# Which engine subtracts the softmax's high parts: GpSimd in place of VectorE, in an attention and feed-forward block

## What is computed

```python
x = x + attention(layernorm(x), ctx)   # 32 heads of 128, 4 key/value heads, 8 query heads on each
x = x + ffn(layernorm(x))              # 512 -> 1376 -> 512, gate and up, weights in 4-bit steps of 32
# attention:
scores = einsum('bhgqk,...', q, k) / sqrt(128)      # keys: 128 of the context, 128 of x
attn = softmax(scores)
out = attn @ v;  return out @ Wo
```

## Time and profile before

| | us |
|---|---|
| device time, median of 3 runs | 816.74 (816.33 to 817.72) |
| the profiled execution | 816.17 |
| its span, first to last instruction | 814.4 |

### The profile page before, as it was taken

The page is one execution under the profiler, slowest core; times in us unless marked ns, Lnnn a source line. Parts: engine busy times, 40 slices in busy tenths (PEclk is TensorE's granted clock), DMA queues, the critical chain, the costliest instruction groups (busy, mean ns, idle before and its releaser), DMA issues.

```text
span 814.4 us, 12628 instructions
## 1 busy us (share of the span) xinstructions
PE 774.8 (95%) x4771; PEld 466.9 (57%) x4771; DVE 599.7 (74%) x1110; ACT 434.0 (53%) x941; POOL 242.9 (30%) x374
## 2 busy tenths in 40 slices
PE   9999999999999999999999999999999999941998
PEld 3446476666666666666666666665544444420445
DVE  5976467788777878767778777898777459989531
ACT  5545447555566655655655555555630019782920
POOL 0720323456334366343456434434300000000000
PEclk9999999999999999999999999999999999985999
DMA  9643145766546666555765547888772000000011
GB/s 319 138 137 117 39 90 133 169 130 156 104 105 159 154 140 145 102 130 122 177 139 137 127 98 136 157 180 150 140 119 46 1 0 1 1 0 0 27 39 39
DMA packets 212044, 87.59 MB, mean 108 GB/s; under 512 B 178832, under 2 KB 195472, under 8 KB 211984
## 3 DMA queue, kind: packets, MB, share of 16 engines
q1 hardware_dynamic: 211984, 86.79, 47.3%
HBM read 31.72 MB, written 10.75 MB: 52 GB/s over the span
## 4 chain that ended last, share of the span: by engine, by line
PE 79%; DVE 10%; DMA 4%; POOL 3%; ACT 2%; issue 1%; SPq 1%; ACTq 0%; DVEq 0%; POOLq 0%
PE bank L338 21%; PE bank L514 12%; PE bank L446 12%; PE bank L430 10%; PE bank L418 9%; PE bank L583 7%; PE bank L450 6%; DVE arena L777 3%; DVE stats L1127 1%; DVE arena L1117 1%; DMA arena<-arena 1%; POOL arena L1204 1%; ACT arena L591 1%; POOL arena L1160 1%; DMA arena<-in_ctx_t 1%
## 5 line engine op out<-in xcount | busy, mean ns | idle before, releaser
L338 PE MATMUL bank<-arena 128*128 128x256 f16 (+1 forms) x1872 | 260.1, 292 | 1.1 <-DVE arena L777 1.1
L338 PEld LDWEIGHTS bank<-arena 128*128 128x128 f16 x1872 | 182.9, 98 | 83.3 <-DVE arena L777 1.3
L1160 POOL TENSOR_SCALAR arena<-arena,rsum 128x256 f32<-128x256 f32 x256 | 133.8, 523 | 288.6 <-DVE rsum L836 274.4
L777 DVE SCALAR_TENSOR_TENSOR arena<-bank,arena 128x512 f16<-128x512 f32 x160 | 109.7, 689 | 113.1 <-ACT arena L591 112.9
L777 DVE SCALAR_TENSOR_TENSOR arena<-arena 128x512 f16<-128x512 f32 (+4 forms) x198 | 171.9, 882 | 19.8 <-ACT arena L591 18.9
L591 ACT ACTIVATE arena<-bank 128x512 f16<-128x512 f32 x160 | 94.7, 596 | 159.0 <-PE bank L430 98.9
L591 ACT ACTIVATE arena<-arena 128x512 f16<-128x512 f32 (+4 forms) x173 | 135.4, 807 | 48.8 <-POOL arena L1190 15.0
L634 ACT ACTIVATE arena<-bank,nmax 128x256 f32<-128x256 f32 x256 | 117.9, 472 | 47.6 <-DVE nmax L828 46.0
L446 PE MATMUL bank<-arena 128*128 128x512 f16 x512 | 121.0, 379 | 0.7 <-ACT arena L591 0.7
L514 PE MATMUL bank<-arena 128*128 128x512 f16 x507 | 109.8, 379 | 0.2 <-DVE stats L1058 0.2
L430 PE MATMUL bank<-arena 128*128 128x512 f16 x384 | 93.4, 379 | 2.5 <-DMA arena<-arena 2.5
(11 more groups left out here) (102 smaller groups left out, 503.8 us busy)
## 6 DMA issues: line engine op xcount, KB each, us to landing
arena<-in_w_units SPq DMA_DIRECT2D x33, 256.0 KB, 3.7
w_ready<-arena SPq DMA_DIRECT2D x33, 256.0 KB, 3.2
arena<-in_wq SPq DMA_DIRECT2D x32, 256.0 KB, 3.4
arena<-in_wo SPq DMA_DIRECT2D x32, 256.0 KB, 3.5
arena<-in_x SPq DMA_DIRECT2D x2, 1024.0 KB, 11.6
out<-arena SPq DMA_DIRECT2D x7, 256.0 KB, 2.0
arena<-arena SPq DMA_TRANSPOSE x72, 4.3
arena<-in_wk SPq DMA_DIRECT2D x4, 256.0 KB, 4.8
```

Source lines behind the costliest of these rows:

```text
L338: last = nc.tensor.matmul(bank, a(i, c), b(j, c), start=start and c == 0 and n == 0, stop=stop and c == chunks - 1 and n == 2)
L777: return nc.vector.scalar_tensor_tensor(out=dst, in0=src, scalar=scale, in1=part, op0=ALU.mult, op1=ALU.subtract)
L1160: done = nc.gpsimd.tensor_scalar(p_s[:, t % 2, :, hh, :], p_s[:, t % 2, :, hh, :], rsum[:, t % 2, hh:hh + 1], P_SCALE, ALU.mult, ALU.mult)
```

## The change

p_lower(t), the subtraction that makes the low part of the probabilities, goes from VectorE's program to GpSimd's. On GpSimd it is a tensor_tensor subtraction (on VectorE it was a multiply by 1.0 and subtract in one instruction, with the same result). For t = 0 it stands in slot 26, in front of normalise(1); for the others at the beginning of GpSimd's step, in front of unit_normalise, unit_dequantise, wq_upper and normalise(t+2). It waits for p_hi, and raises p_lo, as before.

```diff
@@ VectorE @@
-            def p_lower(t):
-                dve.wait_ge(p_hi, t + 1)
-                lo(p_16[:, t % 2, 1, :], p_s[:, t % 2].rearrange("p c h t -> p (c h t)"), p_16[:, t % 2, 0, :], 1.0).then_inc(p_lo, 1)
-
...
-                if slot == 26:
-                    p_lower(0)
...
-                if t + 1 < STEPS:
-                    p_lower(t + 1)
@@ GpSimd @@
+            def p_lower(t):
+
+                pool.wait_ge(p_hi, t + 1)
+                nc.gpsimd.tensor_tensor(p_16[:, t % 2, 1, :], p_s[:, t % 2].rearrange("p c h t -> p (c h t)"), p_16[:, t % 2, 0, :],
+                                        ALU.subtract).then_inc(p_lo, 1)
+
...
                 if slot == 26:
+                    p_lower(0)
                     normalise(1)
...
             for t in range(STEPS):
+                if t + 1 < STEPS:
+                    p_lower(t + 1)
                 for v in units_at(t, 1):
                     unit_normalise(v)
```

## The result

| | us |
|---|---|
| device time before, median of 4 runs on the same chip | 816.89 (816.33 to 817.72) |
| device time after, median of 4 runs | 903.03 (902.53 to 903.74) |
| ratio after to before | 1.106, 95% interval 1.1046 to 1.1073 |
| span of the profiled execution, before and after | 814.4 and 900.8 |

The change costs 86.1 us. Forecast were 922 us, with a range of 896 to 943, so the time lies in the range. The loss forecast was 24% too large (106.7 against 86.1).

The account below looks back on a forecast made before the run. TensorE bounds the kernel now; after the change a closed loop through p_lower and the softmax would. Loop +101.0, last group +3.8, head +1.4 and tail +0.5 sum to +106.7 on 816.17 us: forecast 922 us, range 896 to 943.

Parts of the forecast that it names:

- The bound: Attention steps: TensorE sets the pace at 7.82 us a step through 58 of 64 steps; relieving VectorE there gains nothing.
- The loop: p_upper to next p_upper through p_lower and unit work: 18.10 us a pair of steps against TensorE's 15.63; difference +101.0 us.
- The size of p_lower: GpSimd's 128x1024 subtraction: 2.31 us taken, twice the shortest half-width one, with 1.22 and 2.67 as ends.
- the last group's term: Last head group: ln2_apply on VectorE ahead of the rounding adds 7 times 0.54, +3.8 us taken, between 0 and 3.8.
- The bound from below: Shortest p_lower on GpSimd: 2.1 us if 0.2 of the half-width instruction's 1153 ns were fixed, -12 us in the range.
- wq work: Steps k = 7 to 11 of three groups: stretched normalise 3.3 us a group, wq_upper's queue place 1.3; 13.8 in all.
- Head and tail: Before and after the steady steps: +1.4 us from later normalising and rounding, +0.5 from 2.2 less a 1.7 DMA gain.
- rival 4: TensorE, idle about 2.5 us in 18, is granted only 1.2 GHz: 453 us more, 1270 us; chance 0.03.
- Rival 1: GpSimd's 5.5 us of step work fits under 7.82, so only head and tail pay: 818 us; chance 0.04.
- Rival 2: GpSimd subtracts the wide tile at VectorE's 1.22 us, a pair taking 15.92 us: 858 us; chance 0.05.
- Rival 3: Every p_lower takes 2.67 us through contention between GpSimd and VectorE, 20.9 us more: 943 us; chance 0.08.
- Rival 5: p_lower under 1.08 us leaves TensorE the bound, and relieved VectorE counts in the tail: 814 us; chance 0.02.

Follow-up runs that it names:

- e9: Changed kernel with p_lower(0) and p_lower(59) to p_lower(63) back on VectorE, the 58 between on GpSimd behind the unit work: 816.54 us (1.0006).
- e1: Changed kernel with GpSimd's p_lower(t+1) moved behind unit_normalise and unit_dequantise in its step: 823.94 us (1.0086).
- e10: Kernel before, p_lower still on VectorE, with GpSimd made to wait at each step's head until VectorE's p_lower(t+1) is done: 850.13 us (1.0413).
- e3: Changed kernel with p_lower(t+1) ahead of the unit work in even steps only, behind it in odd steps: 866.40 us (1.0607).

## Why the prediction was right, point by point

- **The bound, and why VectorE's relief gains nothing.** Right on the bound: with p_lower off VectorE in 58 steps, e9 takes the time of before within 0.15%, and TensorE is as busy there as before. That a relief would gain nothing follows from this, but no run shows it by itself, as the exclusion gave VectorE more busy time than the move took.
- **The loop.** Right, link by link. The odd step was worked out as 8.47 and is 8.16, the even one as 9.63 and is 9.24; with wo work 9.07 and 8.76, 10.23 and 9.76. The cover that the prediction named (unit work under p_upper) is what e1 restores.
- **The size of p_lower.** This is the term that was mis-sized. The line of p_lower after, min/median/max in ns:

```profile
L1159 POOL TENSOR_TENSOR arena<-arena x64: 2122/2127/2631, 89.8 to 671.8; 128x1024 f16<-128x1024 f32 x64
```

  Taken were 2.31 us (twice the half width) and 0.08 to the next instruction. Measured are 2.13, and the next one starts 2.08 after p_lower's start (424.30 to 426.38), 0.05 before its end. By the earlier trace rows and this row 512 more columns cost 0.97 us and 0.18 are fixed. That is 0.31 a step (2.31 + 0.08 less 2.08), 58 x 0.31 = 18 us of the 25 by which the 58 steps were forecast too long (556.9, with the last group's term, against 650.45 - 118.35 = 532.1). The even steps' ScalarE copies took 0.08 to 0.15 less (some 3 us), and ln2_apply cost 0.18 and not 0.54 a step, in 4 such turns up to p_upper(60) where 7 were counted (3 us). The bound from below in the prediction, 2.1 us, was the better value. The total came nearer than this term by luck: the steps were 25 us too long in the forecast, head and tail 4.6 too short.
- **wq work.** 4.6 us a group forecast, 4.6 measured (8.79, 10.14, 8.80, 10.14, 9.72 against 8.16 and 9.24). 3.3 of it is the stretched normalise, as forecast. The 1.3 put down to wq_upper's place in the queue have the right size, but another way: the rounding starts as soon as the unit is normalised, and wq_upper beside it then lengthens L853 to 0.72 us, in k = 11 the instruction behind it too (1.09 in place of 0.67).
- **Head and tail.** Forecast +1.4 and +0.5, measured +2.0 (118.35 against 116.36) and +4.5 (900.8 - 650.45 against 814.4 - 568.51). In the tail I had counted on a gain of 1.7, the DMA of p_lower(60) falling from 6.0 to 4.3 us. It took 5.6, behind a p_lower of 2.64 us. The chain after:

```profile
651.59 2.64 POOL arena L1159
654.24 5.64 DMA arena<-arena
...
671.84 2.14 POOL arena L1159
674.00 4.24 DMA arena<-arena
```

  p_lower(60) and its DMA cost 1.1 us on this chain. p_lower(62) shut VectorE's nmax out (1.30 in place of 0.17 us at 664.88) ahead of the last exps, 1.1, and p_lower(63) costs 0.9, of 1.1 forecast. Another 1.3 come from TensorE's clock (rival 4).

  At the head, half of the 2.0 is the forecast's path: behind p_lower(0) and normalise(1) the rounding starts at 95.30 in place of 94.33, v_lo with it, and p_upper(1) comes 1.0 later (110.56 against 109.58). p_lower(0) also held an instruction of unit_scales, and TensorE waited 0.22 us for the v_lo behind it. The other half came one step later and was not forecast: p_lower(1) shut out nmax (0.17 us before), for which the exps wait.

```profile
89.77 2.13 POOL L1159 TENSOR_TENSOR arena<-arena 128x1024 f16<-128x1024 f32 x1 [5.57 <-ACT arena L591]
...
90.15 1.77 DVE L843 TENSOR_SCALAR wscale<-amax 128x16 f32<-128x16 f32 x1
...
112.63 1.20 DVE L828 TENSOR_SCALAR nmax<-nraw 128x4 f32<-128x4 f32 x1
```

- **Rival 1, room on GpSimd.** Refuted for the change, and true for e9.
- **Rival 2, VectorE's pace.** Refuted by the duration. e10 is nearly the kernel that it priced, at VectorE's pace with nothing lost at head and tail: 850 us, where the rival said 858.
- **Rival 3, contention.** The exclusion is real, but p_lower's median shows that it hardly lengthens p_lower where the change puts it. VectorE is its victim (L843 above), and time is lost by it only where something on the chain waits for that instruction: in e3, at the head and in the tail. The forecast looked at the wrong side of it. It named the form with two inputs in SBUF; its own row of 116.89, and most of what was shut out here, are TENSOR_SCALAR instructions.
- **Rival 4, the clock.** TensorE's clock did fall. It cost nothing in the 58 steps, and about 1.3 us in the tail. A short stretch after (length; PE, PEld, DVE, ACT, POOL; PEclk, DMA, GB/s), and TensorE in another:

```profile
450.00:454.00 4.00, 4.00 (x13) 1.62 (x12) 2.07 (x4) 2.55 (x7) 2.68 (x4) 0.59 0.46 140
```

```profile
505.11 3.40 PE L446 MATMUL bank<-arena 128*128 128x512 f16 x8 [2.54 <-ACT arena L591]
```

  Eight matmuls that took 1.89 us take 3.40, at 1.2 GHz, after an idle time of 2.54 us, in some of the steps. The turns of the loop stay at 9.76 and 8.76 us through the stretch at 450, as TensorE is not in the loop. In the tail it is on the chain: the clock was 0.73 of full speed from 678 to 681 us and 0.77 from 681 to 685, behind 1.95 us of idle time, and this group of the last project took 1.9 us before:

```profile
680.67 2.94 PE L446 MATMUL bank<-arena 128*128 128x512 f16 x8
```

- **Rival 5, faster.** Refuted.

What is left open: head and tail were given back together, what a VectorE really relieved would be worth was not tried, and how the exclusion picks the winner when both engines start within 0.05 us was not tried.

## What to carry to other kernels

Before a piece of work goes to the engine with the most idle time, write down what is queued behind its new place and who waits for that, and add up the whole turn from an instruction back to the same one of the next step. If this turn is longer than the bound's step, every step pays, whatever the busy shares say. Here the place in the queue decided between 903 and 824 us with the same instructions. And a long GpSimd instruction on SBUF can stop VectorE's TENSOR_SCALAR on SBUF, even on 4 elements a partition, and its subtraction with both inputs in SBUF. A profile shows that as a longer instruction, as busy time and not as idle time, so a moved instruction need not relieve the engine that it left.

## What the runs showed of the hardware

- A GpSimd subtraction of 128x1024 (float32 less float16, into float16) takes 2.13 us, one of 128x512 1.15 us at least; the unit instruction behind p_lower starts 0.05 us before p_lower's recorded end.
- GpSimd and some of VectorE's instructions exclude each other by whole instructions, both ways: VectorE's 0.43 us rounding took 2.23 beside a whole p_lower and 1.26 beside half of one, a 0.17 us one on 16 elements a partition took 1.77, and GpSimd's 1.15 us took 1.66 behind VectorE's 0.69. This agrees with the Trainium skill (SBUF — State Buffer, section "Who interferes with whom"), which has the first to start hold the shared port pair for its whole instruction. VectorE's reductions kept their 0.69 us when begun inside a p_lower (20 times in e3), and so did its reciprocals (0.18) and its low parts with one input in PSUM (0.69).
- TensorE's granted clock fell to 1.2 GHz for a few us after some idle times of about 2.5 us (0.59 of full speed from 450 to 454 us, behind 2.74 us of idle time) and not after others: from 430 to 440 us, with an idle time of 2.74 us in it, it was 1.00.
